# GNN layer on one Trainium2 core: the weight network's rows made by ScalarE from broadcast edge weights, and all forty sums of a column with sixteen terms

## The chip, the cores and the metric

The kernel runs on one core of one Trainium2 chip. The metric is the device time of one execution in microseconds; each kernel's time is the median of several runs. The profile is one more execution, recorded by the hardware profiler. PE is TensorE, DVE is VectorE, ACT is ScalarE, POOL is GpSimd, SP is SyncE.

## The reference, cut to what matters

The input has 100,000 nodes with 32 features and 25,000 edges sorted by destination. Four layers follow each other; the change touches the first, a message of two feature groups (8 scalars and 8 vectors of 3) whose weights come from a small network of the edge weight:

```python
h      = relu(edge_weight[:, None] @ w1 + b1)   # 25,000 x 64, w1 is 1 x 64
R      = h @ w2 + b2                            # 25,000 x 384: six blocks of 8 x 8 path weights
y      = spherical_harmonics(rel_vec)           # the unit vector n and its products
msg[e] = sum over paths of R * W3J(y) * features[src[e]]   # 32 numbers an edge
out    = segment_sum(msg, dst)
```

The vector output of an edge has a part R·f, a part n (R·s) and a part with the cross product of n and f; f is the source's vectors, s its scalars. Later layers (normalisations, sums over neighbours, an edge network, an attention layer) are the same before and after.

## The kernel before, in words

The edges stand as 128 rows (partitions) by 196 columns. The stage that matters here, the radial stage, goes through them in 7 chunks of 28 columns (`GATHER_CHUNK`), a chunk in 7 passes of the inner loop over i. In this text such a pass is a **block**: four columns, two pairs of two (`slot` 0 and 1), so there are 49 blocks and 98 pairs. One pair goes through four engines:

- DVE, `prepare` (L1633): multiplies the row `w1` (repeated on all partitions, with a zero for the bias row) by the edge weights of two columns, 130 numbers a partition, into `pre`.
- PE, `turn_pre` (L1186): two transposes through the identity (L1119), so that the 65 hidden numbers lie on partitions, into PSUM bank 0 or 1.
- ACT (L884): relu with the bias, PSUM to `hidT`.
- PE, `radial_pair` (L1196, matmul L1202): `hidT` times `w2fold`, 384 path weights for each of two columns, into banks 2 and 3 or 4 and 5. Each float32 matmul shows as two instructions in the profile, each with a weight load.
- DVE: for each column a multiply of 256 path weights by `ff` (16 numbers) and one of 128 weights by the source's 3 x 8 vector numbers (384 products), both at L1365 (a helper's line); then for the pair two sums (`total`, L1376), 32 sums of 16 terms and 96 of 8 terms.

At a chunk's edge DVE forms `ff` and `vec_rows` from the gathered source rows, and at its end it puts the 64 sums of a column together to 32 message numbers, with the cross product made from sums (`g5`, L1786 to L1795). After chunk 4, `make_short` builds an index list for later layers.

POOL meanwhile issues one indirect DMA a column (L665): 56 positions, 140 source rows from the table `x_pos`, 168 destination rows. `keep_to_radial` (L681) holds it back: before every fourth of these, number k, it waits until DVE has finished `int(0.37 * k) - 14` pairs (at most 84, so from k = 265 on nothing holds it). The table `x_pos` is written before by 14 copies of node rows (ACT, `copy_x`, L868 and L869; SP loads and stores, L526 and L531). Six copies stand ahead of the radial loop, the others follow ACT's second relu of a block. POOL's gathers from `x_pos` wait until all are stored. Everything is ordered by hand with semaphores: `pre_ready`, `pre_turned`, `hid_ready`, `radial_ready`, `radial_used`, `prod_used`.

After the last chunk DVE scans the messages into sums (L1464), which the rest of the kernel needs.

## Time and profile before

| | |
|---|---|
| median of 3 runs | 2337.78 us (2337.21 to 2344.02) |
| the profiled execution | 2327.24 us, span 2325.5 us, so 1.7 us lie around the span |
| radial stage, DVE's first product of a chunk to its last chunk's end | 200.8 to 755.2 us |
| busy share of the span | PE 46%, weight loads 32%, DVE 56%, ACT 20%, POOL 57% |
| granted TensorE clock | 0.56 over the span, 0.50 throughout the radial stage (1.2 GHz, the lower of its two levels) |

Rows of the profile give a start, a duration and the idle time of the engine before an instruction, with what ended it. "remote" there is a semaphore whose update comes long after the modelled end of the instruction that makes it.

### The profile page before, as it was taken

How to read it: one execution, taken by the hardware profiler on the slowest of the kernel's cores; microseconds unless marked ns; L12 is line 12 of the kernel's file. 1: busy time of each engine (PE TensorE's matmuls, PEld its weight loads, DVE VectorE, ACT ScalarE, POOL GpSimd, SP SyncE). 2: the span in 40 equal slices, each digit the busy share in tenths (PEclk: the TensorE clock that was granted, in tenths of full speed). 3: DMA queues.
4: the chain of work that ended last, by engine and by line, in shares of the span. 5: the costliest groups of instructions: out<-in, count | busy, mean ns of one | idle time of the engine just before them, and what ended most of it. 6: DMA issues, size and time to landing. Idle time of an engine off the chain costs nothing.

```text
span 2325.5 us, 15151 instructions
## 1 busy us (share of the span) xinstructions
PE 1081.1 (46%) x3970; PEld 738.8 (32%) x3970; DVE 1313.0 (56%) x3018; ACT 472.8 (20%) x949; POOL 1323.8 (57%) x1251
## 2 busy tenths in 40 slices
PE   7706757663641035332233037778426677711222
PEld 3203323331320034332132024444226667611121
DVE  9836878888833925771147933544733677603610
ACT  7522101000000124331123202222101233201200
POOL 8774566561677055067530176666185667773675
PEclk9855555555555567766566555555555555555555
DMA  7155111000000122221014300000000001000000
GB/s 283 25 211 172 45 11 10 10 11 4 11 13 12 61 56 99 91 77 47 28 49 162 102 12 3 11 19 11 25 12 21 23 21 26 24 14 8 9 11 8
DMA packets 65494, 107.52 MB, mean 46 GB/s; under 512 B 33612, under 2 KB 53237, under 8 KB 64628
## 3 DMA queue, kind: packets, MB, share of 16 engines
q1 hardware_dynamic: 24370, 80.77, 9.9%
q0 software_dynamic: 39104, 12.88, 4.2%
q10 hardware_dynamic: 1922, 12.80, 1.4%
q8 instruction: 32, 0.52, 0.1%
q14 instruction: 66, 0.54, 0.1%
HBM read 57.69 MB, written 55.11 MB: 49 GB/s over the span
## 4 chain that ended last, share of the span: by engine, by line
DVE 34%; another core or an unknown queue 21%; PE 19%; issue 17%; POOL 4%; ACT 3%; DMA 2%; DVEq 0%; ACTq 0%; POOLq 0%; PEld 0%; PEldq 0%; SPq 0%
DVE work L1365 11%; DVE work L1376 5%; PE bank L1119 4%; PE bank L1145 3%; DVE A_dst L1365 3%; POOL A_src L665 2%; PE bank L1277 2%; PE bank L1202 2%; DVE stat L1376 2%; PE bank L1270 2%; PE bank L1241 2%; PE bank L1302 1%; POOL A_msg L751 1%; DVE A_msg L1365 1%
## 5 line engine op out<-in xcount | busy, mean ns | idle before, releaser
L665 POOL DMA_INDIRECT A_src<-table,pos_i x392 | 439.0, 1120 | 357.2 <-DMA table<-A_dst 162.5
L1202 PE MATMUL bank<-w2fold,work 65*128 65x384 f32 x392 | 265.8, 856 | 85.9 <-ACT work L884 42.6
L1376 DVE TENSOR_REDUCE work<-work 128x96 f32<-128x768 f32 (+5 forms) x245 | 211.3, 923 | 124.5 <-ACT work L915 77.8
L1119 PE MATMUL bank<-ident,work 128*65 128x128 f32 (+2 forms) x592 | 154.2, 394 | 248.0 <-DVE work L1365 145.2
L665 POOL DMA_INDIRECT A_dst<-in_x,dst_i x196 | 200.2, 1021 | 118.7 <-DVE work L1376 60.8
L804 POOL DMA_INDIRECT out<-A_dst,out_i x196 | 199.8, 1019 | 99.3 <-issue 62.1
L1365 DVE TENSOR_TENSOR work<-bank,work 128x256 f32<-128x256 f32 (+1 forms) x392 | 165.7, 494 | 130.8 <-remote 90.9
L1241 PE MATMUL bank<-nodes_w,small 128*128 128x128 f32 (+1 forms) x784 | 133.4, 338 | 182.5 <-issue 89.1
L665 POOL DMA_INDIRECT A_src<-x_pos,A_tmp x140 | 145.0, 1036 | 100.4 <-DVE work L1376 40.7
L1119 PEld LDWEIGHTS bank<-ident,work 128*65 128x65 f32 (+2 forms) x592 | 104.4, 203 | 307.6 <-issue 160.5
L1241 PEld LDWEIGHTS bank<-nodes_w,small 128*128 128x128 f32 (+1 forms) x784 | 123.6, 246 | 192.4 <-issue 96.3
L1202 PEld LDWEIGHTS bank<-w2fold,work 65*128 65x128 f32 x392 | 123.0, 330 | 186.2 <-issue 135.1
L884 ACT ACTIVATE work<-bank,b1col 65x256 f32<-65x256 f32 x98 | 45.4, 469 | 516.9 <-PE bank L1119 284.4
L1365 DVE TENSOR_TENSOR work<-bank,A_tmp 128x256 f32<-128x256 f32 x49 | 20.6, 420 | 219.1 <-ACT A_tmp L1016 178.1
L1373 DVE SCALAR_TENSOR_TENSOR A_sum<-A_sum,same_pen,bank 128x32 f32<-128x32 f32 x195 | 48.3, 248 | 169.4 <-remote 80.8
L1119 PE MATMUL bank<-ident,end_col 128*32 128x128 f32 (+2 forms) x17 | 6.4, 378 | 285.9 <-DVE end_col L1421 257.0
L1302 PE MATMUL bank<-gw,A_tmp 65*128 65x128 f32 x392 | 94.9, 414 | 80.8 <-ACT A_tmp L1011 45.9
L751 POOL DMA_INDIRECT A_msg<-table,nxt_i x60 | 65.2, 1087 | 108.2 <-DMA table<-A_tmp 75.2
L1302 PEld LDWEIGHTS bank<-gw,A_tmp 65*128 65x128 f32 x392 | 87.6, 322 | 86.1 <-ACT A_tmp L1011 51.1
L1277 PEld LDWEIGHTS bank<-mw,work 65*128 65x128 f32 x392 | 87.1, 327 | 83.4 <-issue 71.8
L757 POOL DMA_INDIRECT edge_sums<-A_sum,out_short x60 | 65.2, 1086 | 80.9 <-DVE A_sum L1365 62.9
L1270 PE MATMUL bank<-work,mw 96*64 96x512 f32 x98 | 95.5, 1078 | 13.3 <-issue 12.8
(355 smaller groups left out, 2267.5 us busy)
## 6 DMA issues: line engine op xcount, KB each, us to landing
work<-in_x SPq DMA_DIRECT2D x26, 960.0 KB
x_pos<-A_sum SPq DMA_DIRECT2D x13, 990.0 KB
out<-work ACTq DMA_DIRECT2D x13, 960.0 KB
table<-A_dst SPq DMA_DIRECT2D x2, 3136.0 KB
edge_sums<-A_dst SPq DMA_DIRECT2D x2, 3136.0 KB
table<-A_dst SPq DMA_DIRECT2D x14, 448.0 KB
A_src<-table,pos_i POOLq DMA_INDIRECT x392
A_tmp<-in_edge_attr_2x SPq DMA_DIRECT2D x49, 112.0 KB
```

The costliest lines, as they stand in the source:

```text
L665: pool.indirect_dma_start(out=column(t), out_offset=None, in_=of, in_offset=bass.IndirectOffsetOnAxis(ap=idx[:, t:t + 1], axis=0), bounds_ ...
L751: return lambda t: pool.indirect_dma_start(out=column(t), out_offset=None, in_=of, in_offset=bass.IndirectOffsetOnAxis(ap=idx[:, t:t + 1], ...
L804: pool.indirect_dma_start(out=out, out_offset=bass.IndirectOffsetOnAxis(ap=out_i[:, t:t + 1], axis=0), in_=A_dst[:, t, :], in_offset=None, ...
L1119: return nc.tensor.transpose(out_ap, in_ap, ident[0:n, 0:n])
L1145: last = nc.tensor.matmul(banks[6 + h][:, 0:half], lo_hot[:, 2 * slot + j, :], hi_hot[:, 2 * slot + j, h * half:(h + 1) * half], start=Fal ...
L1202: last = nc.tensor.matmul(banks[2 + 2 * slot + j][:, 0:PATHS], hidT[:, slot, j * P:(j + 1) * P], w2fold[:], start=True, stop=True)
L1241: last = nc.tensor.matmul(banks[2 + 2 * w + s][0:parts, k * P:(k + 1) * P], n_xT[:, s, k * parts:(k + 1) * parts], nodes_w[:, w * P:(w + 1 ...
L1270: nc.tensor.matmul(banks[2 + slot][0:HID0, :], mw1[:], catT[:, slot, :], start=True, stop=True).then_inc(e_h, 1)
L1277: last = nc.tensor.matmul(banks[4 + slot][:, j * FEAT:(j + 1) * FEAT], hidT2[:, slot, j * P:(j + 1) * P], mw2[:], start=True, stop=True)
L1302: last = nc.tensor.matmul(banks[2 + slot][:, j * P:(j + 1) * P], catT3[:, slot, j * P:(j + 1) * P], gw2[:], start=True, stop=True)
L1365: return v.tensor_tensor(out=o, in0=a, in1=b, op=op)
L1376: return v.tensor_reduce(out=o, in_=a, axis=AX, op=op)
```

## The change

The edge weights are transposed once, after the histogram (two PE transposes into banks 0 and 1, two ACT copies, two DMAs to a table `ew_turned_rows` of 196 x 128 in DRAM). For each block ACT then issues one DMA that reads 512 edge weights and spreads them over 65 partitions (`load_ew`, three buffers ahead), and its relu takes them from SBUF with `w1` as a scale for each partition. `prepare`, `turn_pre`, `pre` and their two semaphores are gone. DVE multiplies the first 256 weights of both columns of a pair in one instruction, the cross product is formed from the source's vectors at the start of a chunk, and the 40 sums of a column, all of 16 terms, are made by one instruction a pair. The diff, cut to its core:

```diff
+EW_SLOTS = 3
...
+        ew_turned_rows = dram("ew_turned_rows", (T, P))
...
-        w1rep = sb("w1rep", [P, HID0 + 1])
+        w1col = sb("w1col", [HID0 + 1, 1])
...
-        banks = [ctx.enter_context(nc.psum_tensor(f"bank_{b}", [P, 512], f32)) for b in range(8)]
+        all_banks = ctx.enter_context(nc.psum_tensor("bank", [P, 8, 512], f32))
+        banks = [all_banks[:, b, :] for b in range(8)]
...
-        pre = cv(P, SLOTS, 2, HID0 + 1)
         hidT = cv(HID0 + 1, SLOTS, 2 * P)
         prod = cv(P, 4, 640)
-        path_sums = cv(P, GATHER_CHUNK, 64)
+        path_sums = cv(P, GATHER_CHUNK, 40)
         ff = cv(P, GATHER_CHUNK, 16)
-        g5 = cv(P, GATHER_CHUNK, 8, 5)
-        vec_a, vec_rows = cv(P, GATHER_CHUNK, 24), cv(P, GATHER_CHUNK, 24)
+        g5_words = cv(P, GATHER_CHUNK, 80)
+        g5 = g5_words.rearrange("p t (i k v) -> p t i k v", i=5, k=2)
+        vec_a = cv(P, GATHER_CHUNK, 24)
+        ew_rows = flat(prod)[:, 0:2 * P].rearrange("p (b e) -> p b e", b=2)
...
+            act.wait_ge(ew_turned, 1)
+            nc.scalar.copy(ew_rows[:, 0, :], banks[0][:, 0:P])
+            nc.scalar.copy(ew_rows[0:T - P, 1, :], banks[1][0:T - P, 0:P]).then_inc(ew_copied, 1)
+            act.wait_ge(ew_copied, 1)
+            act.dma_start(ew_turned_rows[0:P, :], ew_rows[:, 0, :]).then_inc(ew_stored, 16)
+            act.dma_start(ew_turned_rows[P:T, :], ew_rows[0:T - P, 1, :]).then_inc(ew_stored, 16)
+
+            def load_ew(q):
+                act.dma_start(ew_all[:, q % EW_SLOTS, :], ew_turned_rows[4 * q:4 * q + 4, :].rearrange("t p -> (t p)")
+                              .partition_broadcast(HID0 + 1)).then_inc(ew_in[q % EW_SLOTS], 16)
+
+            act.wait_ge(ew_stored, 32)
+            act.wait_ge(pos_f_ready, 1)
+            for q in range(EW_SLOTS):
+                load_ew(q)
             copies = list(range(D_CHUNKS + 1))
             for _ in range(COPIES_FIRST[0]):
                 copy_x(copies.pop(0))
@@ -879,10 +901,14 @@
             act.sem_inc(hid_ready, SLOTS)
             for u in range(T // 2):
                 slot = u % SLOTS
-                act.wait_ge(pre_turned, u + (1 + SLOTS))
+                q = u // 2
+                act.wait_ge(ew_in[q % EW_SLOTS], 16 * (q // EW_SLOTS + 1))
                 act.wait_ge(radial_ready, u + 1)
-                nc.scalar.activation(hidT[:, slot, :], banks[slot][0:HID0 + 1, 0:2 * P], ACT.Relu,
-                                     bias=b1col[:]).then_inc(hid_ready, 1)
+                nc.scalar.activation(hidT[:, slot, :], ew_all[:, q % EW_SLOTS, slot * 2 * P:(slot + 1) * 2 * P], ACT.Relu,
+                                     bias=b1col[:], scale=w1col[:]).then_inc(hid_ready, 1)
+                if slot == 1 and q + EW_SLOTS < QUADS:
+                    act.wait_ge(hid_ready, u + 1 + SLOTS)
+                    load_ew(q + EW_SLOTS)
...
+            pe.wait_ge(loaded_edges, 96)
+            turn(banks[0][:, 0:P], ew[:, 0:P], P)
+            turn(banks[1][0:T - P, 0:P], ew[:, P:T], P).then_inc(ew_turned, 1)
...
-            def turn_pre(u, slot):
-                pe.wait_ge(pre_ready, u + 1)
-                pe.wait_ge(hid_ready, u + 1)
-                for j in range(2):
-                    last = turn(banks[slot][0:HID0 + 1, j * P:(j + 1) * P], pre[:, slot, j, :], P)
-                last.then_inc(pre_turned, 1)
-
-            turn_pre(0, 0)
-            turn_pre(1, 1)
...
-                for slot in range(SLOTS):
-                    turn_pre(i * 2 + (2 + slot), slot)
...
-            def prepare(u_next, slot, t):
-
-                v.wait_ge(pre_turned, u_next + 1)
-                tt(pre[:, slot], mid(w1rep[:], 2), bcast(ew[:, bass.ds(t, 2)], HID0 + 1), ALU.mult).then_inc(pre_ready, 1)
...
+                def n_rows(k):
+                    return bcast(unit[:, cols, k:k + 3], 8)
+
+                def f_rows(k):
+                    return g5[:, :, k:k + 3, 0, :]
+
+                by_row, crossed = vec_in.rearrange("p t v i -> p t i v"), g5[:, :, 0:3, 1, :]
+                a4r = vec_a.rearrange("p t (i v) -> p t i v", i=3)
                 step(tt(a4, vec_in, n3, ALU.mult))
                 v.tensor_copy(ff[:, :, 0:8], A_src[:, cols, 0:8])
-                v.tensor_copy(vec_rows.rearrange("p t (i v) -> p t i v", i=3), vec_in.rearrange("p t v i -> p t i v"))
+                v.tensor_copy(f_rows(0), by_row)
+                v.tensor_copy(g5[:, :, 3:5, 0, :], by_row[:, :, 0:2, :])
                 step(total(ff[:, :, 8:16], a4))
+                step(tt(crossed, n_rows(1), f_rows(2), ALU.mult))
+                step(tt(a4r, n_rows(2), f_rows(1), ALU.mult))
+                step(tt(crossed, crossed, a4r, ALU.subtract))
                 for i in range(GATHER_CHUNK // 4):
                     for slot in range(SLOTS):
                         u = i * 2 + (c * GATHER_CHUNK // 2 + slot)
-                        t_in, t = i * 4 + 2 * slot, i * 4 + (c * GATHER_CHUNK + 2 * slot)
-                        prepare(u + 2, slot, t + 4)
+                        t_in = i * 4 + 2 * slot
                         v.wait_ge(radial_ready, u + (1 + SLOTS))
                         v.wait_ge(prod_used, u + 1)
+                        at, two = bass.ds(t_in, 2), all_banks[:, 2 + 2 * slot:4 + 2 * slot, :]
+                        to = prod[:, 2 * slot:2 * slot + 2, :]
+                        tt(to[:, :, 0:256].rearrange("p j (a b) -> p j a b", b=16),
+                           two[:, :, 0:256].rearrange("p j (a b) -> p j a b", b=16),
+                           ff[:, at, :].unsqueeze(2).to_broadcast([P, 2, 16, 16]), ALU.mult)
                         for j in range(2):
-                            bank, to = banks[2 + 2 * slot + j], prod[:, 2 * slot + j, :]
-                            tt(to[:, 0:256].rearrange("p (a b) -> p a b", b=16),
-                               bank[:, 0:256].rearrange("p (a b) -> p a b", b=16),
-                               ff[:, bass.ds(t_in + j, 1), :].to_broadcast([P, 16, 16]), ALU.mult)
-                            vec = vec_rows[:, bass.ds(t_in + j, 1), :].rearrange("p a (i v) -> p (a i) v", i=3)
-                            last = tt(to[:, 256:640].rearrange("p (a i v) -> p a i v", i=3, v=8),
-                                      bank[:, 256:384].rearrange("p (a v) -> p a v", v=8).unsqueeze(2)
-                                      .to_broadcast([P, 16, 3, 8]),
-                                      vec.unsqueeze(1).to_broadcast([P, 16, 3, 8]), ALU.mult)
+                            rows_j = g5_words[:, bass.ds(t_in + j, 1), 0:48].rearrange("p a (i b) -> p (a i) b", b=16)
+                            last = tt(to[:, j, 256:640].rearrange("p (u i b) -> p u i b", i=3, b=16),
+                                      two[:, j, 256:384].rearrange("p (u b) -> p u b", b=16).unsqueeze(2)
+                                      .to_broadcast([P, 8, 3, 16]),
+                                      rows_j.unsqueeze(1).to_broadcast([P, 8, 3, 16]), ALU.mult)
                         last.then_inc(radial_used, 1)
                     for slot in range(SLOTS):
                         v.wait_ge(radial_used, i * 2 + (c * GATHER_CHUNK // 2 + slot + 1 + SLOTS))
                         at, mine = bass.ds(i * 4 + 2 * slot, 2), prod[:, 2 * slot:2 * slot + 2, :]
-                        total(path_sums[:, at, 0:16], mine[:, :, 0:256].rearrange("p j (a b) -> p j a b", b=16))
-                        last = total(path_sums[:, at, 16:64], mine[:, :, 256:640].rearrange("p j (a b) -> p j a b", b=8))
-                        last.then_inc(prod_used, 1)
+                        total(path_sums[:, at, :], mine.rearrange("p j (a b) -> p j a b", b=16)).then_inc(prod_used, 1)
                 v.wait_ge(prod_used, (c + 1) * GATHER_CHUNK // 2 + SLOTS)
 
-                beta = path_sums[:, :, 16:40].rearrange("p t (u i) -> p t u i", i=3)
-                gamma = path_sums[:, :, 40:64].rearrange("p t (u i) -> p t u i", i=3)
-
-                def n_at(k):
-                    return unit[:, cols, k:k + 3].unsqueeze(2).to_broadcast([P, GATHER_CHUNK, 8, 3])
-
-                vec_out = A_msg[:, cols, 8:32].rearrange("p t (u i) -> p t u i", i=3)
+                n_first = unit[:, cols, 0:3].unsqueeze(2).to_broadcast([P, GATHER_CHUNK, 8, 3])
                 v.tensor_copy(A_msg[:, cols, 0:8], path_sums[:, :, 0:8])
-                v.tensor_copy(g5[:, :, :, 0:3], gamma)
-                step(v.tensor_copy(g5[:, :, :, 3:5], gamma[:, :, :, 0:2]))
-                step(tt(a4, n_at(1), g5[:, :, :, 2:5], ALU.mult))
-                step(tt(vec_out, beta, a4, ALU.add))
-                step(tt(a4, n_at(2), g5[:, :, :, 1:4], ALU.mult))
-                step(tt(vec_out, vec_out, a4, ALU.subtract))
-                step(tt(a4, n_at(0), bcast(path_sums[:, :, 8:16], 3), ALU.mult))
-                step(tt(vec_out, vec_out, a4, ALU.add))
+                step(tt(a4, n_first, bcast(path_sums[:, :, 8:16], 3), ALU.mult))
+                step(tt(A_msg[:, cols, 8:32], path_sums[:, :, 16:40], vec_a, ALU.add))```

On PE, at the start of the radial loop, the order before was (turns into banks 0 and 1, then four products into banks 2 to 5, and so on; a row is a source line, an operation, what it writes and reads, the shape, and the semaphores that it waits for):

```order
L1119 MATMUL bank_0<-ident,work 65x128 [waits hid_ready,pre_ready,pos_int]
L1119 MATMUL bank_0<-ident,work 65x128
L1119 MATMUL bank_1<-ident,work 65x128 [waits hid_ready,pre_ready]
L1119 MATMUL bank_1<-ident,work 65x128
L1202 MATMUL bank_2<-w2fold,work 128x384 [waits radial_used,hid_ready]
L1202 MATMUL bank_3<-w2fold,work 128x384
L1202 MATMUL bank_4<-w2fold,work 128x384 [waits radial_used,hid_ready]
L1202 MATMUL bank_5<-w2fold,work 128x384
```

and at the same place the changed kernel has:

```order
L1220 MATMUL bank<-w2fold,work 128x384 [waits radial_used,hid_ready,pos_int]
L1220 MATMUL bank<-w2fold,work 128x384
L1220 MATMUL bank<-w2fold,work 128x384 [waits radial_used,hid_ready]
L1220 MATMUL bank<-w2fold,work 128x384
L1220 MATMUL bank<-w2fold,work 128x384 [waits radial_used,hid_ready]
```

The turns have left PE's queue, so the four products of a block follow those of the block before directly.

On DVE, one block in the loop before (`work` holds `pre`, `prod` and the sums; `w1rep` marks `prepare`):

```order
L1365 TENSOR_TENSOR work<-bank_2,work 128x256 [waits prod_used,radial_ready]
L1365 TENSOR_TENSOR work<-bank_2,work 128x384
L1365 TENSOR_TENSOR work<-bank_3,work 128x256
L1365 TENSOR_TENSOR work<-bank_3,work 128x384
L1365 TENSOR_TENSOR work<-w1rep,A_msg 128x130 [waits pre_turned]
L1365 TENSOR_TENSOR work<-bank_4,work 128x256 [waits prod_used,radial_ready]
L1365 TENSOR_TENSOR work<-bank_4,work 128x384
L1365 TENSOR_TENSOR work<-bank_5,work 128x256
L1365 TENSOR_TENSOR work<-bank_5,work 128x384
L1376 TENSOR_REDUCE work<-work 128x2x16 [waits radial_used]
L1376 TENSOR_REDUCE work<-work 128x2x48
```

and in the changed kernel, from the start of chunk 0 through its first block:

```order
L1381 TENSOR_TENSOR work<-A_src,A_tmp 128x672 [waits dve_seq,src_rows_0]
L1768 COPY work<-A_src 128x28x8 [waits dve_seq]
L1769 COPY work<-A_src 128x28x3x8
L1770 COPY work<-A_src 128x28x2x8
L1392 TENSOR_REDUCE work<-work 128x28x8
L1381 TENSOR_TENSOR work<-A_tmp,work 128x28x3x8 [waits dve_seq]
L1381 TENSOR_TENSOR work<-A_tmp,work 128x672 [waits dve_seq]
L1381 TENSOR_TENSOR work<-work 128x28x3x8 [waits dve_seq]
L1381 TENSOR_TENSOR work<-bank,work 128x2x256 [waits prod_used,radial_ready,dve_seq]
L1381 TENSOR_TENSOR work<-bank,work 128x384 x2
L1381 TENSOR_TENSOR work<-bank,work 128x2x256 [waits prod_used,radial_ready]
L1381 TENSOR_TENSOR work<-bank,work 128x384 x2
```

A block has gone from 14 instructions (two `prepare`, eight products, four sums) to 8 (six products, two sums), and three products have come to the chunk's start while four products and two copies have left its end.

On ACT, the first relus before (A_sum<-small and A_sum<-work are `copy_x`, here of node chunk 6):

```order
L884 ACTIVATE work<-bank_0,b1col 65x256 [waits loaded_w,radial_ready,pre_turned]
L884 ACTIVATE work<-bank_1,b1col 65x256 [waits radial_ready,pre_turned]
L868 COPY A_sum<-small 128x60 [waits x_stored_0,x_loaded_0]
L869 COPY A_sum<-work 128x60x32
L884 ACTIVATE work<-bank_0,b1col 65x256 [waits radial_ready,pre_turned]
```

and in the changed kernel:

```order
L907 ACTIVATE work<-A_tmp,b1col,w1col 65x256 [waits loaded_w,radial_ready,ew_in_0]
L907 ACTIVATE work<-A_tmp,b1col,w1col 65x256 [waits radial_ready,ew_in_0]
L886 DMA A_tmp<-ew_turned_rows 65x512 [waits hid_ready]
L875 COPY A_sum<-small 128x60 [waits x_stored_0,x_loaded_0]
L876 COPY A_sum<-work 128x60x32
L907 ACTIVATE work<-A_tmp,b1col,w1col 65x256 [waits radial_ready,ew_in_1] x2
```

The relu no longer waits for `pre_turned`, but for the DMA of its edge weights, and the copy of node chunk 6 is no longer behind a turn that waits for DVE.

## Rows read from the trace of the kernel before

**Rows 1.** The page: busy time of the engines in the span

```profile
PE 1081.1 (46%) x3970; PEld 738.8 (32%) x3970; DVE 1313.0 (56%) x3018; ACT 472.8 (20%) x949; POOL 1323.8 (57%) x1251
```

**Rows 2.** Timeline of DVE, one block: start, us, what, count [idle before]

```profile
214.38 0.29 DVE L1365 TENSOR_TENSOR work<-w1rep,A_msg 128x130 f32<-128x130 f32 x1
214.58 1.69 DVE L1365 TENSOR_TENSOR work<-bank,work 128x256 f32<-128x256 f32 x4
216.18 0.30 DVE L1365 TENSOR_TENSOR work<-w1rep,A_msg 128x130 f32<-128x130 f32 x1
216.38 1.69 DVE L1365 TENSOR_TENSOR work<-bank,work 128x256 f32<-128x256 f32 x4
217.97 3.00 DVE L1376 TENSOR_REDUCE work<-work 128x32 f32<-128x512 f32 x4
220.87 0.30 DVE L1365 TENSOR_TENSOR work<-w1rep,A_msg 128x130 f32<-128x130 f32 x1
```

**Rows 3.** Timeline of PE, the same block

```profile
209.62 1.10 PE L1119 MATMUL bank<-ident,work 128*65 128x128 f32 x4
210.81 5.49 PE L1202 MATMUL bank<-w2fold,work 65*128 65x384 f32 x8
```

**Rows 4.** Timeline of DVE at the edge between chunks 0 and 1

```profile
247.00 0.28 DVE L1786 COPY A_msg<-work 128x224 f32<-128x224 f32 x1
...
247.61 0.42 DVE L1788 COPY work<-work 128x448 f32<-128x448 f32 x1
248.06 0.86 DVE L1365 TENSOR_TENSOR work<-A_tmp,work 128x672 f32<-128x672 f32 x1
...
254.50 0.63 DVE L1751 COPY work<-A_src 128x672 f32<-128x672 f32 x1
255.93 0.29 DVE L1365 TENSOR_TENSOR work<-w1rep,A_msg 128x130 f32<-128x130 f32 x1
```

**Rows 5.** Timeline of ACT up to the radial loop's first block

```profile
114.94 0.30 ACT L868 COPY A_sum<-small 128x60 f32<-128x60 f32 x1 [26.36 <-DMA small<-pos_table]
...
196.89 0.47 ACT L884 ACTIVATE work<-bank,b1col 65x256 f32<-65x256 f32 x1 [49.24 <-PE bank L1119]
...
198.77 1.79 ACT L869 COPY A_sum<-work 128x1920 f32<-128x1920 f32 x1
```

**Rows 6.** Timeline of POOL: starts and ends of its trains of gathers

```profile
246.08 1.00 POOL L665 DMA_INDIRECT A_src<-x_pos,A_tmp  x1 [20.11 <-DMA x_pos<-A_sum]
...
569.75 0.99 POOL L665 DMA_INDIRECT A_dst<-in_x,dst_i  x1 [44.38 <-DVE work L1376]
...
619.47 0.99 POOL L665 DMA_INDIRECT A_dst<-in_x,dst_i  x1 [1.81 <-DVE work L1376]
...
751.91 1.48 POOL L665 DMA_INDIRECT A_dst<-in_x,dst_i  x1 [0.30 <-issue]
```

**Rows 7.** Busy time in one stretch: PE, PEld, DVE, ACT, POOL, clock, DMA share, GB/s

```profile
246.00:621.00 375.00, 224.21 (x425) 114.94 (x424) 306.38 (x690) 32.26 (x70) 214.56 (x209) 0.50 0.09 10
```

**Rows 8.** Timeline of all engines but POOL, one block of chunk 6

```profile
667.20 1.68 DVE L1365 TENSOR_TENSOR work<-bank,work 128x256 f32<-128x256 f32 x4 [11.31 <-remote]
...
683.31 0.47 ACT L884 ACTIVATE work<-bank,b1col 65x256 f32<-65x256 f32 x1 [24.77 <-remote]
...
688.91 0.47 ACT L884 ACTIVATE work<-bank,b1col 65x256 f32<-65x256 f32 x1 [5.13 <-issue]
...
689.43 2.93 PE L1202 MATMUL bank<-w2fold,work 65*128 65x384 f32 x4 [2.67 <-issue]
...
699.40 1.68 DVE L1365 TENSOR_TENSOR work<-bank,work 128x256 f32<-128x256 f32 x4 [15.79 <-remote]
...
710.60 1.69 DVE L1365 TENSOR_TENSOR work<-bank,work 128x256 f32<-128x256 f32 x4 [9.32 <-remote]
...
716.90 0.47 ACT L884 ACTIVATE work<-bank,b1col 65x256 f32<-65x256 f32 x1 [27.52 <-remote]
```

**Rows 9.** Timeline of DVE: the first instruction after the radial stage

```profile
755.23 14.84 DVE L1464 TENSOR_TENSOR_SCAN A_sum<-same,A_msg 128x196 f32<-128x196 f32 x32
```

More of the change, by code:

```diff
@@ L234, in gnn_kernel @@
         weights_folded, cw_done = sem("weights_folded"), sem("cw_done")
[L235 removed]
+        ew_turned, ew_copied, ew_stored = sem("ew_turned"), sem("ew_copied"), sem("ew_stored")
+        ew_in = [sem(f"ew_in_{k}") for k in range(EW_SLOTS)]
         hid_ready, radial_ready, radial_used = sem("hid_ready"), sem("radial_ready"), sem("radial_used")
```

24 lines of the change are left out of this document (12 added, 12 removed).

## The prediction

> **What bounds the kernel now.** I looked first at the page for the busy shares [rows 1]: no engine is above 57%, so waits decide, and a gain must be sought in the stage that the change touches. The chain of waits runs through the radial stage from the first product at 200.8 us to the last chunk's end at 755.2 [rows 9]. The work after it starts from DVE's sums, so what counts is when DVE gets there.
>
> The timeline shows three regimes. In the first, undisturbed one, DVE starts a block every 6.49 us (214.38 to 220.87) with no idle row between [rows 2], and PE needs nearly as much, 5.49 + 1.10 us [rows 3]. DVE sets the pace, PE follows closely. In the second, POOL is held back by DVE: of the 375 us from 246 to 621 it is busy 214.6 with 209 gathers, each with 0.30 us of issue, 277 us together [rows 7], so it stands still for 98, of which 44.4 are `make_short` [rows 6]. In the third, POOL has long issued without a pause, and PE and with it DVE creep. The last train of gathers runs from 619.5 to 753.4 [rows 6]. DVE waits for a product from 655.9 to 667.2, 36 us into it, and a block that took 6.49 us then takes 33.6 (683.31 to 716.90, relu to relu) [rows 8]. PE has started its products within 1 us of the relu (689.43, until 692.4 by the modelled ends), but their semaphores come late. I read the time of each PE group off who is released: turn of slot 1 at 688.91 (5.6 us after that of slot 0), product of slot 0 at 699.40 (10.5), of slot 1 at 710.60 (11.2), next turn at 716.90 (6.3). A turn group is two matmul instructions, a product group four: 2.8 us for each, 12 in a block, 33.6 us. So in a creeping block the price is per PE instruction. DVE's and ACT's own work is hidden in it.
>
> **The change part by part.**
>
> *DVE, inside a block.* The four products of a slot take 1.60 us (214.58 to 216.18) [rows 2]; their 1280 numbers at 0.96 a ns would be 1.33, which leaves 0.065 for each instruction. A `prepare` costs 0.20 (214.38 to 214.58), the four sums 2.90 (217.97 to 220.87), 2.67 for the 2560 numbers and 0.058 each. The change removes two `prepare` (0.40), two products' overhead (0.13) and two sums' overhead (0.12), with the same numbers multiplied and summed: 0.65 us a block, 5.84 instead of 6.49. That the first product now spans two PSUM banks is not in the trace. From below its price is nothing; from above I take that the merging saves nothing, 0.13 us a block. I take nothing, as both sizes of product [rows 2] already run at the same rate from one bank. The Trainium skill (VectorE: DVE Perf Modes, The TRN2 errata) gives VectorE 120 cycles as the fixed part of an instruction with a PSUM source and 58 with an SBUF source. By it the two merged products would save 0.25 us a block, 6 us more over 49 blocks. The row disagrees, with 0.065.
>
> *DVE, at a chunk's edge.* Now 8.93 us (247.00 to 255.93): three copies, six products of 0.86 (0.89 with the gap) for the messages, one product, two copies and a sum at the start [rows 4]. After: one copy (0.2) and two products (1.8) at the end; at the start one product (0.9), copies (0.2, 0.55 and 0.4, by the copies of 672 and 448 numbers in the same rows), the sum (0.88) and three products (2.7). Together 7.6, so 1.3 less an edge. At the last chunk only the end counts, 6.4 before and 2.0 after.
>
> *PE.* Without the turns a block is 8 matmul instructions instead of 12. In the undisturbed regime that is 5.5 us under DVE's 5.84, hidden. In a creeping block, 8 x 2.8 = 22.4 us instead of 33.6.
>
> *ACT.* The relu of 0.47 us [rows 8] reads SBUF instead of PSUM, and each block has one more DMA issue. Two relus and a copy of node rows (1.79) [rows 5] fill 2.7 of a block's 6.49 us, so the rest costs nothing while it stays under 3 us a block. The loads run three blocks ahead, 17 us, and would have to be later than that to be felt. The preamble (two turns, two copies, DMAs) falls into the 26.4 us for which ACT waits for the position table until 114.94 [rows 5]. Nothing for it; without that cover, each us of it would delay the copies by one.
>
> *The start of the loop.* The first relus no longer hang on a turn that waits for DVE. ACT stood for 49.2 us before 196.89 [rows 5]; now both relus and node chunk 6's copy, which stood at 198.77, go when PE reaches its loop, some 20 us earlier, and the later copies follow blocks of 5.84 instead of 6.49 us. The last copy then comes 6 to 8 us earlier, and with it the first gather from `x_pos`, now at 246.08 and released by that store [rows 6]. **−7 us.** The first product itself moves by less than 1: three more products at the chunk's start (2.7 us) take the place of two `prepare` and two waits for PE.
>
> *246 to 621 us.* DVE's work falls by 35 x 0.65 + 5 x 1.3 = 29 us. But POOL needs 14/0.37 = 38 gathers of 1.32 us (277/209) for a chunk's 14 pairs, 50 us, where DVE needs 7 x 6.49 + 8.9 = 54.3 now and 48.5 after. The faster DVE frees POOL of part of its 54 us of pauses outside `make_short`, and after that POOL is the pace, and without pauses PE creeps sooner. The bounds are 0 and 5 x 4.3 = 22. I take 8, near the lower end, because of the creeping. **−8 us.**
>
> *The last train.* Before, from 619.5: an edge, four blocks at 6.49, then 93 us (655.9 to 748.8) of creeping for three blocks, and the last edge to 755.2 [rows 8, 9]. After: four blocks save 2.6, the edge 1.3, the end 4.4, 8 together; the creeping blocks at 22.4 save up to 3 x 11.2 = 34. Bounds 8 and 42. I take **−30**, nearer the upper end, because removed PE instructions are counted by the row at full price, but less than all of it, because creeping may begin earlier in this train. POOL's own end moves by 15, to 738. The scan and the layer norm's first chunks (755.2 on) need its rows only later, so it does not decide.
>
> Sum: −7 − 8 − 30 = −45 us. The profiled execution's 2327.2 us becomes 2282; it stands 10.5 under the median of the runs, so on their scale I expect 2337.8 − 45 = 2293 us.
>
> **The rivals.**
>
> *POOL sets the pace.* The price of creeping hangs on POOL's issue and not on the number of PE instructions (33.6 us a block stays; that two kinds of group gave the same 2.8 us speaks against it). Then the last train gives 8 and the middle 0 to 8: −7 − 8 − 0 to 8 = 15 to 23 us, with noise 10 to 30. 2308 to 2328. Chance 0.23. The Trainium skill (SBUF — State Buffer, Who interferes with whom) says that PE and ACT never wait on anyone; the trace differs, since PE's completions are late only while POOL issues without pause [rows 8].
>
> *Creeping goes away.* With a third fewer PE instructions it starts later or not at all. Then POOL's 308 gathers from 239 on (407 us) and `make_short` (44) end near 690, 63 us earlier, and DVE, which is needed alone, can be done up to 50 us before that: 60 to 115 us, 2223 to 2278. For it speaks that creeping came only 36 us into the last train; against it, that PE still does two thirds of the work. Chance 0.13.
>
> *Slower: more blocks creep.* POOL's pauses are what ended the creeping. DVE's speed takes them away, and a block that moves from 5.84 to 33.6 us at the old price costs 27.8. Against the 15 to 23 us of the POOL case one such block makes it 5 to 13 us slower, two 33 to 41: 2343 to 2379. It decides from the first such block on. At the new price (16.6 a block) it would need three. Chance 0.12.
>
> *The change does nothing that can be told*, within 0.3% (7 us, about what a measurement of this kernel can tell from no change): would come about if a small gain of the POOL case and part of a creeping block cancel. Chance 0.09.
>
> **How the numbers follow.** The forecast's own case, 30 to 60 us faster (2278 to 2308), has 0.43. The range from 2245 to 2332 holds it, the POOL case, most of the near half of the third and a part of no change: about 0.8. Faster by over 0.3%: 0.43 + 0.23 + 0.13 = 0.79; same 0.09; slower 0.12.
>
> **What would show it.** In the changed profile: blocks 5.84 us apart on DVE while POOL pauses, with sums of 1.39 us; edges of 7.6 us; the first gather from `x_pos` near 239; relu to relu of a creeping block 22 us (33 would refute the price per instruction); a last train from about 605, with DVE's scan near 710. ACT waiting for `ew_in` anywhere, or a wide product above 0.72 us, would refute the parts costed at nothing. The forecast fails if the number of creeping blocks changes by more than one, which nothing in the rows fixes.

## The result, and the profile after

The changed kernel takes 2276.38 us (median of 4 runs, 2258.58 to 2300.15), the kernel before 2340.9 beside it; the ratio is 0.9695, 95% interval 0.9621 to 0.977. (Ratios here and below leave out runs that are more than 1.5% above the fastest of the same kernel, here the one of 2300.15 us.) From profile to profile it is 2327.24 to 2269.11 us, 58 less, and by the medians 64.5; 45 were forecast.

The page of the changed kernel, first the busy times, then three groups (columns as in [rows 1]):

```profile
PE 1028.1 (45%) x3772; PEld 691.5 (31%) x3772; DVE 1271.8 (56%) x2708; ACT 487.2 (21%) x951; POOL 1316.4 (58%) x1251
...
L1392 DVE TENSOR_REDUCE work<-work 128x80 f32<-128x1280 f32 (+3 forms) x147 | 204.8, 1424 | 125.9 <-issue 96.0
...
L1381 DVE TENSOR_TENSOR work<-bank,work 128x384 f32<-128x384 f32 (+1 forms) x294 | 155.0, 594 | 111.9 <-remote 77.0
...
L907 ACT ACTIVATE work<-A_tmp,b1col,w1col 65x256 f32<-65x256 f32 x98 | 58.7, 600 | 430.1 <-PE bank L1220 195.6
```

The relu takes 0.60 us where it took 0.47, and no wait before it is put down to the loads of edge weights. The timeline of DVE through the last train of gathers (start, duration, what, and the idle time before it with its releaser):

```profile
598.76 0.28 DVE L1800 COPY A_msg<-work 128x224 f32<-128x224 f32 x1
...
606.34 3.15 DVE L1381 TENSOR_TENSOR work<-bank,work 128x512 f32<-128x512 f32 x6
609.40 2.87 DVE L1392 TENSOR_REDUCE work<-work 128x80 f32<-128x1280 f32 x2
612.19 3.14 DVE L1381 TENSOR_TENSOR work<-bank,work 128x512 f32<-128x512 f32 x6
...
640.10 1.62 DVE L1381 TENSOR_TENSOR work<-bank,work 128x512 f32<-128x512 f32 x3 [6.12 <-remote]
...
661.21 1.62 DVE L1381 TENSOR_TENSOR work<-bank,work 128x512 f32<-128x512 f32 x3 [9.63 <-remote]
...
683.61 1.62 DVE L1381 TENSOR_TENSOR work<-bank,work 128x512 f32<-128x512 f32 x3 [9.57 <-remote]
...
690.02 15.83 DVE L1480 TENSOR_TENSOR_SCAN A_sum<-same,A_msg 128x196 f32<-128x196 f32 x31
706.68 0.57 DVE L1480 TENSOR_TENSOR_SCAN A_sum<-same,A_msg 128x196 f32<-128x196 f32 x1 [0.83 <-issue]
711.63 0.35 DVE L1437 COPY end_col<-A_sum 128x32 f32<-128x32 f32 x1 [4.39 <-remote]
713.55 0.41 DVE L1441 TENSOR_TENSOR_SCAN seam_state<-rows,bank 32x128 f32<-32x128 f32 x1 [1.57 <-DVE end_col L1437]
```

Read against [rows 2, 4, 8, 9]: an edge of 7.58 us (598.76 to 606.34) instead of 8.93, a block of 5.85 (606.34 to 612.19) instead of 6.49, a creeping block of 22.4 (661.21 to 683.61) instead of 33.6, and the end of the radial stage at 690.0 instead of 755.2. Last, most of the small steps behind the scans wait 1.0 to 1.6 us first; before it was 0.7 us at most, as these rows of the kernel before show:

```profile
770.11 0.18 DVE L1421 COPY end_col<-A_sum 128x32 f32<-128x32 f32 x1
770.85 0.41 DVE L1425 TENSOR_TENSOR_SCAN seam_state<-rows,bank 32x128 f32<-32x128 f32 x1 [0.56 <-PE bank L1119]
```

The start of the loop and of the trains, from the timelines of ACT, DVE and POOL of the changed kernel:

```profile
186.85 1.09 ACT L907 ACTIVATE work<-A_tmp,b1col,w1col 65x256 f32<-65x256 f32 x2 [31.14 <-PEq L1211]
...
188.52 1.79 ACT L876 COPY A_sum<-work 128x1920 f32<-128x1920 f32 x1
...
199.29 0.86 DVE L1381 TENSOR_TENSOR work<-A_src,A_tmp 128x672 f32<-128x672 f32 x1 [0.24 <-DVE gb1c L1385]
...
245.34 0.99 POOL L672 DMA_INDIRECT A_src<-x_pos,A_tmp  x1 [17.65 <-DMA x_pos<-A_sum]
...
597.60 0.99 POOL L672 DMA_INDIRECT A_dst<-in_x,dst_i  x1 [3.43 <-issue]
...
780.69 0.99 POOL L758 DMA_INDIRECT A_msg<-table,nxt_i  x1 [44.05 <-DMA table<-A_tmp]
```

The busy times of the stage behind, 690.0 to 780.7 of the changed kernel and 755.2 to 828.6 of the kernel before (POOL's first gather for the next stage):

```profile
690.00:780.70 90.70, 3.00 (x12) 2.28 (x13) 69.85 (x107) 13.70 (x18) 37.24 (x32) 0.50 0.19 64
```

```profile
755.20:828.60 73.40, 2.99 (x12) 2.26 (x13) 68.79 (x107) 13.81 (x18) 0.02 (x1) 0.50 0.18 72
```

DVE has the same 107 instructions and 69 to 70 us of work, but needs 90.7 us instead of 73.4: POOL's train runs on until 736.6 beside it, where before it ended at 753.4, ahead of the scans. So the 65.2 us won by the end of the radial stage are partly given back:

| stretch | before, us | after, us | difference | forecast |
|---|---|---|---|---|
| until the first `x_pos` gather | 246.1 | 245.3 | -0.8 | -7 |
| to the last train's start | 373.4 | 352.3 | -21.1 | -8 |
| to the end of the radial stage | 135.7 | 92.4 | -43.3 | -30 |
| to the next stage's first gather | 73.4 | 90.7 | +17.3 | 0 |
| the rest of the span | 1496.9 | 1486.2 | -10.7 | 0 |

The rest is the same code; no row names a cause for its 10.7 us, and they are less than the 41.6 us over which the changed kernel's own runs spread. The second of the five stretches in busy times, the kernel before first:

```profile
246.00:619.40 373.40, 222.61 (x423) 114.24 (x422) 304.81 (x687) 32.26 (x70) 213.33 (x207) 0.50 0.09 10
```

```profile
245.30:597.60 352.30, 194.11 (x284) 87.26 (x284) 274.78 (x467) 41.38 (x69) 211.44 (x207) 0.50 0.14 23
```

DVE works 30.0 us less there and stands idle 8.9 us more (77.5 instead of 68.6).

### The profile page after: what moved, and what is told of

Its sections match the earlier page's. It is cut to its first block, busy times and chain, and to the rows that moved or that the text cites. A ratio compares the mean times of both kernels' runs of the same rounds, so it can differ in the third digit from the quotient of the medians.

```text
span 2266.9 us, 14390 instructions
## 1 busy us (share of the span) xinstructions
PE 1028.1 (45%) x3772; PEld 691.5 (31%) x3772; DVE 1271.8 (56%) x2708; ACT 487.2 (21%) x951; POOL 1316.4 (58%) x1251
## 4 chain that ended last, share of the span: by engine, by line
DVE 16%; PE 13%; another core or an unknown queue 13%; issue 11%; POOL 2%; ACT 2%; DMA 1%; DVEq 0%; ACTq 0%; POOLq 0%; SPq 0%
PE bank L1145 3%; DVE work L1381 3%; PE bank L1293 3%; PE bank L1286 3%; PE bank L1318 1%; DVE stat L1392 1%; DVE A_dst L1381 1%; DVE A_sum L1480 1%; POOL A_msg L758 1%; PE bank L1341 1%; POOL A_src L672 1%; DVE A_msg L1381 1%; DVE r L1392 1%; DVE A_sum L1389 1%
## 5 line engine op out<-in xcount | busy, mean ns | idle before, releaser
L672 POOL DMA_INDIRECT A_src<-table,pos_i x392 | 429.6, 1096 | 356.3 <-DMA table<-A_dst 164.4
L1220 PE MATMUL bank<-w2fold,work 65*128 65x384 f32 x392 | 270.4, 866 | 188.9 <-DVE work L1381 124.5
L1392 DVE TENSOR_REDUCE work<-work 128x80 f32<-128x1280 f32 (+3 forms) x147 | 204.8, 1424 | 125.9 <-issue 96.0
L672 POOL DMA_INDIRECT A_dst<-in_x,dst_i x196 | 203.9, 1040 | 107.6 <-issue 65.5
L1220 PEld LDWEIGHTS bank<-w2fold,work 65*128 65x128 f32 x392 | 121.9, 329 | 335.6 <-issue 335.5
L1257 PE MATMUL bank<-nodes_w,small 128*128 128x128 f32 (+1 forms) x784 | 135.8, 341 | 184.7 <-ACT small L931 111.9
L1381 DVE TENSOR_TENSOR work<-bank,work 128x384 f32<-128x384 f32 (+1 forms) x294 | 155.0, 594 | 111.9 <-remote 77.0
L672 POOL DMA_INDIRECT A_src<-x_pos,A_tmp x140 | 144.5, 1032 | 89.8 <-issue 47.8
L907 ACT ACTIVATE work<-A_tmp,b1col,w1col 65x256 f32<-65x256 f32 x98 | 58.7, 600 | 430.1 <-PE bank L1220 195.6
L1145 PE MATMUL bank<-ident,end_col 128*32 128x128 f32 (+2 forms) x17 | 6.4, 378 | 300.9 <-DVE end_col L1437 280.0
L1145 PE MATMUL bank<-ident,work 128*128 128x128 f32 (+1 forms) x392 | 89.9, 372 | 114.6 <-ACTq L920 61.5
L1381 DVE TENSOR_TENSOR work<-bank,A_tmp 128x256 f32<-128x256 f32 x49 | 20.6, 420 | 205.1 <-ACT A_tmp L1042 167.9
L758 POOL DMA_INDIRECT A_msg<-table,nxt_i x60 | 67.2, 1121 | 80.2 <-DMA table<-A_tmp 44.1
L1145 PEld LDWEIGHTS bank<-ident,work 128*128 128x128 f32 (+1 forms) x392 | 66.2, 193 | 120.2 <-issue 71.9
```

The source lines that it names most:

```text
L672: pool.indirect_dma_start(out=column(t), out_offset=None, in_=of, in_offset=bass.IndirectOffsetOnAxis(ap=idx[:, t:t + 1], axis=0), bounds_ ...
L758: return lambda t: pool.indirect_dma_start(out=column(t), out_offset=None, in_=of, in_offset=bass.IndirectOffsetOnAxis(ap=idx[:, t:t + 1], ...
L1145: return nc.tensor.transpose(out_ap, in_ap, ident[0:n, 0:n])
L1220: last = nc.tensor.matmul(banks[2 + 2 * slot + j][:, 0:PATHS], hidT[:, slot, j * P:(j + 1) * P], w2fold[:], start=True, stop=True)
L1257: last = nc.tensor.matmul(banks[2 + 2 * w + s][0:parts, k * P:(k + 1) * P], n_xT[:, s, k * parts:(k + 1) * parts], nodes_w[:, w * P:(w + 1 ...
L1381: return v.tensor_tensor(out=o, in0=a, in1=b, op=op)
```

## The experiments

Twelve measurements follow: nine variants, one of them taken twice (half_weights and half_again), and the two kernels once more. "Creeping" is the state in which an engine's instructions or their semaphores come far later than their own durations explain. What nobody had forecast came first: the kernel before, beside them, took 1909.6 us (23 runs) and 1915.3 (11) on two chips, and 2312.6 (11) and 2307.1 (13) on two others. On the first two no creeping shows in the seven traces taken there (no wait of any engine ends with "remote"); on the others it does, as where the result was measured. I call them **quiet** and **creeping** chips. Ratios are to the kernel before on the same chip.

### Quiet chips: the halves, and the price of PE's instructions

**rows_alone**, the kernel before with ScalarE's rows alone:

```diff
-            turn_pre(0, 0)
...
-                        prepare(u + 2, slot, t + 4)
...
+                nc.scalar.activation(hidT[:, slot, :], ew_all[:, q % EW_SLOTS, slot * 2 * P:(slot + 1) * 2 * P], ACT.Relu,
+                                     bias=b1col[:], scale=w1col[:]).then_inc(hid_ready, 1)
```

> The kernel before with the first half of the change alone: ScalarE makes the rows from broadcast edge weights, no prepare and no turns, 8 PE matmul instructions a block; the products, the 16- and 8-term sums and the cross product at a chunk's end stay as before. If creeping is priced per PE instruction (2.8 us each): an undisturbed block takes 6.49 - 0.40 = 6.09 us, a creeping one 22.4, and most of the gain is here: 35 to 55 us under the kernel before (ratio 0.976 to 0.985). If the gain of the whole change is DVE's shorter work and creeping follows POOL alone: creeping blocks stay at 33.6 us and the gain is at most 49 x 0.40 = 20 us (ratio 0.991 or above).

Measured: 0.9896 (0.9864 to 0.9928), blocks 6.09 us apart.

**sums_alone**, with DVE's arithmetic alone:

```diff
...
-                        total(path_sums[:, at, 0:16], mine[:, :, 0:256].rearrange("p j (a b) -> p j a b", b=16))
-                        last = total(path_sums[:, at, 16:64], mine[:, :, 256:640].rearrange("p j (a b) -> p j a b", b=8))
-                        last.then_inc(prod_used, 1)
+                        total(path_sums[:, at, :], mine.rearrange("p j (a b) -> p j a b", b=16)).then_inc(prod_used, 1)
```

> The kernel before with the second half alone: wide products, one sum a pair, cross product at the chunk's start; prepare and the turns stay, so 12 PE matmul instructions a block. Price per PE instruction: undisturbed block 6.49 - 0.25 = 6.24 us, edge 7.6, creeping block still 33.6; the gain is 4 x 0.25 + 1.3 + 4.4 = 7 us in the last train and up to 15 in the middle: 5 to 22 us (ratio 0.990 to 0.998). If DVE's shorter work carries the change: 40 us or more (0.983 or less).

Measured: 0.996 (0.9922 to 0.9998), blocks 6.25 us apart at the start of a chunk, then 6.47. There PE, which still has its twelve instructions, has become the pace:

```profile
218.96 5.49 PE L1204 MATMUL bank<-w2fold,work 65*128 65x384 f32 x8
224.24 1.13 PE L1121 MATMUL bank<-ident,work 128*65 128x128 f32 x4
225.43 5.49 PE L1204 MATMUL bank<-w2fold,work 65*128 65x384 f32 x8
```

**turns_unused**, the changed kernel with four PE transposes a block that nothing reads or waits for:

```diff
                     last.then_inc(radial_ready, 1)
+                for slot in range(SLOTS):
+                    for j in range(2):
+                        turn(banks[slot][:, j * P:(j + 1) * P], ident[:], P)
```

> The changed kernel with four transposes of a constant a block put back on PE, two after each other slot's products, into banks 0 and 1 which nothing reads; they wait for nothing, signal nothing, and nothing waits for them. Price per PE instruction: a creeping block goes back from 22 to 33.6 us and the time to within 20 us of the kernel before (ratio to it 0.990 to 1.0); undisturbed blocks at about 6.5 us, since PE then needs 5.5 + 1.1. Price per group with a semaphore: creeping blocks stay at 22 us and the ratio to the kernel before stays at 0.970 to 0.978.

Measured: 0.9837 (0.9772 to 0.9902), blocks of 5.84 to 5.97 us.

**half_weights**, the changed kernel with hidden rows and path weights in fp16, so that a product is one PE instruction:

```diff
-        w2fold = sb("w2fold", [HID0 + 1, PATHS])
+        w2fold = sb("w2fold", [HID0 + 1, PATHS], f16)
...
-        hidT = cv(HID0 + 1, SLOTS, 2 * P)
+        hidT = cv(HID0 + 1, SLOTS, 2 * P, dt=f16)
```

> The changed kernel with the hidden rows and the folded weights held in fp16, so that a product is one PE instruction instead of two: 4 a block (the rounding of these two operands is all that changes in what is computed). Price per PE instruction: a creeping block takes 11.2 us, and the time falls by 15 to 45 us more under the changed kernel (less than 3 x 11.2 + the middle's share, because POOL's gathers then bind). Price per group with a semaphore: creeping blocks stay at 22 us and the time stays within 0.5% of the changed kernel's.

Measured: 0.989 (0.9809 to 0.9971), blocks of 5.84 us.

What follows: DVE sets the pace of a block in the kernel before, in rows_alone and in the changed kernel, and my terms for it hold (0.40 and 0.24 us for the two halves). In sums_alone PE takes over at 6.47 us after three blocks, so the second half pays in full only when the turns are gone too. In the changed kernel four PE instructions more cost at most 0.13 us a block, and four fewer change nothing that can be told. Of creeping these four say nothing, since there was none; both branches of what I expected of it stay open.

### Quiet chips: where DVE's time goes

**before_again** and **after_again** are the two kernels unchanged, for their traces.

> The kernel before, unchanged, for its trace beside the kernels of this call. The four experiments above ran where the kernel before takes 1910 us and no wait of 8 us in the radial stage shows. If creeping belongs to the program, this trace shows it again, with blocks of 33.6 us and about 2335 us in all. If it belongs to where the program runs, this trace shows 49 blocks of 6.49 us, edges of 8.9, a radial stage of about 49 x 6.49 + 6 x 8.9 + 6.4 + make_short, 380 to 400 us, and about 1910 us in all.

> The changed kernel, unchanged, beside it. Without creeping its radial stage is shorter by 49 x 0.65 + 6 x 1.3 + 4.4 = 44 us, but the gathers (1.30 us each, 308 of them, 401 us from the first x_pos gather) then end later than DVE's last chunk: if the stage behind needs them, only part of the 44 comes through, 30 to 35 us (ratio 0.981 to 0.985). If nothing waits for POOL, all 44 (0.977). With creeping: 0.9695 again.

**plain_dst** takes 168 of the 196 gathers of destination rows out of POOL's train; six plain DMAs bring other rows in their place, so the kernel's result is another:

```diff
-            gather_dst(range(DST_FIRST * GATHER_CHUNK, T), keep_to_radial)
+            for c in range(DST_FIRST, CHUNKS):
+                pool.dma_start(A_dst[:, c * GATHER_CHUNK:(c + 1) * GATHER_CHUNK, :],
+                               x[0:P * GATHER_CHUNK, :].rearrange("(p t) f -> p t f", t=GATHER_CHUNK)
+                               ).then_inc(dst_rows[c], 16)
...
```

> The changed kernel with 168 of the 196 gathers of destination rows left out; six plain DMAs bring other rows in their place, so what the four layers compute from the destination's own features is another value. POOL's last train has no gathers then. With creeping: the last chunks run undisturbed, 5.84 us a block, the radial stage ends 50 us or more earlier than in the changed kernel, and no seam step is slow. Without creeping: the radial stage keeps its length, and the time shows what the gathers cost behind it: nothing if they are hidden, up to 100 us if POOL is what the first sums and the short gathers wait for.

Measured: before_again 1901.47 us; after_again 0.9849 (0.9802 to 0.9896); plain_dst 0.9613 (0.9562 to 0.9665). Timelines, first before_again: the two pauses of POOL and its first gather of the next stage, and DVE's end of the radial stage.

```profile
474.38 0.99 POOL L665 DMA_INDIRECT A_dst<-in_x,dst_i  x1 [28.89 <-DVE work L1376]
480.88 0.99 POOL L665 DMA_INDIRECT A_dst<-in_x,dst_i  x1 [1.60 <-DVE work L1376]
...
680.60 0.99 POOL L751 DMA_INDIRECT A_msg<-table,nxt_i  x1 [17.50 <-DMA table<-A_tmp]
...
575.68 9.79 DVE L1464 TENSOR_TENSOR_SCAN A_sum<-same,A_msg 128x196 f32<-128x196 f32 x21
```

The same of after_again, and from DVE the second small step behind the scans and a wait for gathered destination rows:

```profile
448.12 0.99 POOL L672 DMA_INDIRECT A_dst<-in_x,dst_i  x1 [3.57 <-DVE work L1392]
453.95 0.99 POOL L672 DMA_INDIRECT A_dst<-in_x,dst_i  x1 [0.95 <-DVE work L1392]
...
661.31 0.99 POOL L758 DMA_INDIRECT A_msg<-table,nxt_i  x1 [17.43 <-DMA table<-A_tmp]
...
534.83 10.71 DVE L1480 TENSOR_TENSOR_SCAN A_sum<-same,A_msg 128x196 f32<-128x196 f32 x23
...
550.45 0.41 DVE L1441 TENSOR_TENSOR_SCAN seam_state<-rows,bank 32x128 f32<-32x128 f32 x1 [0.56 <-PE bank L1145]
...
645.26 1.09 DVE L1381 TENSOR_TENSOR A_dst<-A_dst,A_sum 128x896 f32<-128x896 f32 x1 [30.87 <-DMA A_dst<-in_x,dst_i]
```

And of plain_dst:

```profile
607.27 1.07 POOL L761 DMA_INDIRECT A_msg<-table,nxt_i  x1 [205.77 <-DMA table<-A_tmp]
...
533.87 11.63 DVE L1483 TENSOR_TENSOR_SCAN A_sum<-same,A_msg 128x196 f32<-128x196 f32 x25
```

DVE ends the radial stage 40.9 us earlier, the next stage's first gather comes only 19.3 earlier. Behind the radial stage POOL's gathers are what is late: DVE waits for their rows (30.87 us at 645.26 of after_again); without them it ends the radial stage at the same time (533.9), and the next stage starts 54 us sooner. POOL's pauses shrink by 26.0 us (30.5 to 4.5), since DVE reaches the awaited pairs sooner; its 129 gathers behind them take 190 us instead of 182, and 19 remain.

### Creeping chips: the pauses, and the price of an instruction

**before_free** and **after_free** leave out POOL's waits, each in its kernel:

```diff
-                if k % 4 == 0 and need > 0:
-                    pool.wait_ge(prod_used, need + SLOTS)
```

> The kernel before without keep_to_radial's waits: POOL issues its gathers without a pause. Where no creeping shows: the pauses of 28.9 and 1.6 us (445.5 to 474.4 and 479.3 to 480.9) go, the last destination row is gathered near 632 instead of 663, and if POOL is what the stage behind waits for, the kernel is 25 to 30 us faster (ratio 0.984 to 0.987). If DVE is what sets the pace there, 0 to 5 us. Where creeping shows: longer trains make more blocks creep, 33.6 us each, and it is slower by 50 us or more.

> The changed kernel without keep_to_radial's waits. Where no creeping shows and POOL sets the time behind the radial stage: the pauses of 3.6 and 1.0 us go, the last gather of destination rows ends near 639 less the little that slower gathers at chunk edges cost, and the time is that of the kernel before without these waits, within 0.5%: the gain of the change there came through shorter pauses of POOL and is gone when there are none. If DVE's shorter radial stage itself carries the gain: the two stay 20 to 30 us apart. Where creeping shows: slower than the changed kernel by 30 us or more.

Measured: before_free 1.0795 (1.075 to 1.0839), after_free 1.0445 (1.0406 to 1.0484), so 180 and 96 us slower than the kernel before there. POOL issues its 308 gathers in one train (256.1 to 662.3 and 251.7 to 658.0), and nearly everything in it creeps. The relus of before_free, timeline of ACT:

```profile
486.12 0.47 ACT L882 ACTIVATE work<-bank,b1col 65x256 f32<-65x256 f32 x1 [27.53 <-remote]
...
519.72 0.47 ACT L882 ACTIVATE work<-bank,b1col 65x256 f32<-65x256 f32 x1 [27.53 <-remote]
...
553.32 0.47 ACT L882 ACTIVATE work<-bank,b1col 65x256 f32<-65x256 f32 x1 [27.53 <-issue]
```

Of after_free:

```profile
577.05 0.60 ACT L905 ACTIVATE work<-A_tmp,b1col,w1col 65x256 f32<-65x256 f32 x1 [10.60 <-remote]
588.25 0.60 ACT L905 ACTIVATE work<-A_tmp,b1col,w1col 65x256 f32<-65x256 f32 x1 [10.60 <-issue]
599.45 0.60 ACT L905 ACTIVATE work<-A_tmp,b1col,w1col 65x256 f32<-65x256 f32 x1 [10.60 <-remote]
```

Block to block that is 33.60 us with 12 PE matmul instructions and 22.40 with 8: 2.80 each, twice. But the change also took two of four semaphore groups away, so a price for something in a group is not excluded yet. turns_free settles that: the changed kernel without POOL's waits, with the four transposes of turns_unused.

> turns_unused without keep_to_radial's waits (the changed kernel with four transposes of a constant a block that nothing reads or waits for). Where creeping shows: price per PE instruction gives 12 x 2.80 = 33.6 us for a block, although only two groups carry semaphores; price per group with a semaphore gives 22.4 as in the changed kernel without these waits. Where no creeping shows: blocks of 5.84 to 5.97 us, as in turns_unused.

Measured (one run): 2445.5 us, against 2408.1 for after_free, on another creeping chip. The relus:

```profile
516.20 0.60 ACT L905 ACTIVATE work<-A_tmp,b1col,w1col 65x256 f32<-65x256 f32 x1 [10.60 <-remote]
...
538.60 0.60 ACT L905 ACTIVATE work<-A_tmp,b1col,w1col 65x256 f32<-65x256 f32 x1 [21.80 <-remote]
549.80 0.60 ACT L905 ACTIVATE work<-A_tmp,b1col,w1col 65x256 f32<-65x256 f32 x1 [10.60 <-remote]
```

33.60 us again (516.20 to 549.80), although nothing waits for the four transposes and none carries a semaphore: 11.2 us for four instructions that are done in 1.06. The price is per PE instruction.

**half_again** is half_weights once more; **half_free** leaves out POOL's waits as well.

> half_weights once more (fp16 hidden rows and weights, one PE instruction a product, 4 a block, POOL held back as in the changed kernel). In the two kernels without POOL's waits a creeping block took 33.60 us with 12 instructions and 22.40 with 8: 2.80 each. Where creeping shows, a creeping block should take 4 x 2.80 = 11.2 us, and the last train and the middle lose most of what creeping still costs the changed kernel: 25 to 55 us under its 2276 (ratio to the kernel before 0.948 to 0.962). If something else holds a slot's round at 11.2 us (the semaphores between PE, ACT and DVE), the blocks stay at 22.4 and the ratio at 0.965 to 0.975. Where no creeping shows: 0.985 to 0.99, as for half_weights.

> half_weights without keep_to_radial's waits. Where creeping shows: creeping blocks of 11.2 us, 33 of them in POOL's 401 us train, so that DVE and POOL end the radial stage together near 650 to 670, and no train is left that slows the steps behind; 2210 to 2260 us if the kernel before takes 2340, so this would beat both kernels. If blocks stay at 22.4 us it is as slow as the changed kernel without these waits, ratio 1.04. Where no creeping shows: as half_weights, within 0.5%.

Measured: half_again 0.9656 (0.9598 to 0.9715), half_free 1.0082 (1.0031 to 1.0134). Creeping blocks take 11.20 us, as in these relus of half_free, two slots each:

```profile
527.52 0.60 ACT L905 ACTIVATE work<-A_tmp,b1col,w1col 65x256 f16<-65x256 f32 x1 [6.40 <-issue]
531.73 0.60 ACT L905 ACTIVATE work<-A_tmp,b1col,w1col 65x256 f16<-65x256 f32 x1 [3.60 <-PE bank L1218]
538.72 0.60 ACT L905 ACTIVATE work<-A_tmp,b1col,w1col 65x256 f16<-65x256 f32 x1 [6.40 <-PE bank L1218]
```

The blocks are as expected, but they don't measure PE's price at four instructions: the relus are 4.21 and 6.99 us apart, which is three and five instructions of 1.40 us, as DVE has them (three products; three products and two sums), where two PE groups of two would give 5.6 and 5.6. DVE's eight instructions make 11.2 us as well. The times are not as expected. DVE's timeline of half_again shows why:

```profile
641.57 4.71 DVE L1480 TENSOR_TENSOR_SCAN A_sum<-same,A_msg 128x196 f32<-128x196 f32 x10
646.95 0.57 DVE L1480 TENSOR_TENSOR_SCAN A_sum<-same,A_msg 128x196 f32<-128x196 f32 x1 [0.67 <-issue]
648.35 0.57 DVE L1480 TENSOR_TENSOR_SCAN A_sum<-same,A_msg 128x196 f32<-128x196 f32 x1 [0.83 <-issue]
649.75 0.57 DVE L1480 TENSOR_TENSOR_SCAN A_sum<-same,A_msg 128x196 f32<-128x196 f32 x1 [0.83 <-issue]
```

Ten scans go at full speed, then each starts 1.40 us after the last, though it takes 0.57 and no releaser shows: creeping holds DVE too, at 1.40 us an instruction. PE's 2.80 for a matmul fits that, a matmul and its weight load being two instructions. The radial stage ends at 641.6, but the 32 scans then end near 677 and the small steps behind begin at 686.2, where the kernel before needs 14.9 us for the scans [rows 9]. In half_free DVE reaches its final scans only at 793.8, with POOL done at 659: a chunk's edge takes 21.7 us (relu to relu, 388.94 to 410.62), and `make_short`, mostly small instructions, stretches from 30 us between its first and last scan (401.9 to 432.1 in after_again) to 97.5 (593.7 to 691.2). So half_again is not shown to be faster than the changed kernel (the intervals overlap), and half_free is slower. No version here is shown to beat both.

## Why the prediction was right, and where its sizes were off

**DVE in a block and at an edge**: 5.85 and 7.58 us where 5.84 and 7.6 were forecast. The merged product over two banks saves its overhead as assumed. The halves, each alone, gave 0.40 and 0.24 us, the second only where PE was not the pace. By the 120 cycles that the Trainium skill (VectorE: DVE Perf Modes, The TRN2 errata) gives for a PSUM source, the merged products would have saved 0.25 us instead of 0.13, and so the second half 0.37; the trace does not agree, with its 0.24, here as in [rows 2].

**The price per PE instruction**: confirmed on creeping chips, 12, 8 and again 12 instructions at 2.80 us. At four it was not measured, since DVE's eight instructions took as long. The rival *POOL sets the pace* (33.6 stays) is refuted by the 22.4 of the changed kernel. That a group or a semaphore is priced is refuted by turns_free.

**The last train**: -43.3, just past the upper bound of 42. The number of creeping blocks stayed at three, and they took 58.3 us instead of 93.3: 34.9 saved, where 3 x 11.2 is 33.6. I had taken off for creeping that begins earlier in the train; it began after four undisturbed blocks, as before.

**The middle**: -21.1 where I took 8, near the upper bound of 22. The term was mis-sized. DVE's work fell by 30.0 us, as forecast (29), and only 8.9 came back as idle time. POOL stood still 79 us instead of 98 (352.3 less 207 gathers of 1.32). I had also read this stretch as free of creeping, which it was not, before as after; from the timeline of DVE of the kernel before:

```profile
294.84 1.69 DVE L1365 TENSOR_TENSOR work<-bank,work 128x256 f32<-128x256 f32 x4 [11.32 <-remote]
```

How much of the 21.1 us is the lower price of such blocks was not separated.

**The start**: -0.8 instead of -7. ACT's copy did move, from 198.77 to 188.52, but DVE reached its first chunk at 199.29 instead of 195.31. The small steps ahead creep, and where there is no creeping the two kernels reach that point within 0.5 us (152.04 and 151.62). The last copy, which follows DVE's blocks, stood at 242.53 instead of 243.70. The step failed because I read those steps as fixed. Whether ACT's new DMAs make them slower was not tried.

**The end**: I let POOL's own end not count. It counts: the train outlives the radial stage by 46.6 us, and DVE's steps beside it creep, 17.3 us in all. From the first scan to the first layer norm it is 34.5 us (690.02 to 724.48), against 21.3 in the kernel before (755.23 to 776.52), and 21.3 again in after_again (534.83 to 556.12), where POOL's train runs beside them too but nothing creeps. So it is creeping, not the train as such, that costs there. That is the missing term. With it the forecast sum would have been -28; the larger savings in the middle and the last train and the unexplained 10.7 outweighed it, so 2293 against 2276 is partly luck of signs.

**ACT at nothing**: right. Its relu is 0.13 us longer and no wait for `ew_in` shows.

**The rival on the other side**, one more creeping block in the last train, did not come. That the chip decides whether anything creeps stood in neither forecast nor rivals; on a quiet chip the change gives 1.5%, by another way: POOL's gathers end 19 us sooner.

## What to carry to other kernels

A saving in the radial stage was partly lost wherever POOL's train outlived it: read what the faster engine's successor waits for, and whether a long train of gathers still runs there. When waits show as late semaphores while nothing is busy, count instructions of the slowed engines, scans and small steps too, rather than their durations. And compare on more than one chip: this change is worth 3.0% on one kind and 1.5% on the other.
